# An attention kernel in which SyncE, not ScalarE, sends the rows of the maximum, the loop over pairs of images is written out, and the projections stand earlier

## What is computed

```python
h = group_norm(x) * gamma + beta                 # 32 groups of 4 channels
q, k, v = wq @ h + bq, wk @ h + bk, wv @ h + bv  # 128 x 1024 each
w = softmax(q.T @ k * scale, axis=-1)            # 1024 x 1024
x = x + wo @ (v @ w.T) + bo
```

## Time and profile before

| | us |
|---|---|
| median of 3 runs | 2451.29 |
| lowest and highest run | 2448.13, 2462.1 |
| the profiled execution's own time | 2444.07 |
| its span, first to last instruction | 2442.4 |

### The profile page before, as it was taken

How to read it: one execution, slowest core, us unless ns; L and a number is a source line. 1 busy time by engine, 2 the same in 40 slices (tenths; PEclk the granted TensorE clock), 3 DMA queues, 4 the chain that set the end, 5 groups by cost and what they waited for, 6 DMA issues and landing times. The chain is left out here.

```text
span 2442.4 us, 32992 instructions
## 1 busy us (share of the span) xinstructions
PE 2197.5 (90%) x11778; PEld 1067.0 (44%) x11778; DVE 1726.8 (71%) x2115; ACT 1661.2 (68%) x3009; POOL 458.7 (19%) x682
## 2 busy tenths in 40 slices
PE   1899899989998898999899988999887999999999
PEld 0333333333333333333333333333333888888887
DVE  0777768767776767677677867676752777777776
ACT  0366667656666666666666666676665888888887
POOL 4102020111202020201112020201101333333331
PEclk7789889989989998989899988998996999999999
DMA  7224151505234251605053351515101111111111
GB/s 143 29 47 69 37 81 38 90 23 83 45 60 62 44 76 30 97 21 90 25 80 54 51 72 33 85 34 91 25 16 47 57 41 63 62 54 40 62 50 46
DMA packets 63660, 137.36 MB, mean 56 GB/s; under 512 B 14880, under 2 KB 26272, under 8 KB 63392
## 3 DMA queue, kind: packets, MB, share of 16 engines
q1 hardware_dynamic: 60064, 133.90, 29.8%
q10 hardware_dynamic: 3456, 1.57, 0.4%
HBM read 57.31 MB, written 22.02 MB: 32 GB/s over the span
## 5 line engine op out<-in xcount | busy, mean ns | idle before, releaser
L473 DVE TENSOR_REDUCE h_half_nmax<-h_s_ps 128x2 f32<-128x1024 f32 x1024 | 1207.1, 1220 | 382.7 <-PE h_s_ps L660 378.4
L591 ACT ACTIVATE h_probs<-h_st_ps 128x512 f32<-128x512 f32 x2048 | 1070.5, 601 | 480.5 <-PE h_st_ps L764 448.5
L764 PE MATMUL h_st_ps<-h_qrep,h_krep 51*128 51x512 f32 x2048 | 690.0, 505 | 132.9 <-ACT h_probs L591 112.7
L764 PEld LDWEIGHTS h_st_ps<-h_qrep,h_krep 51*128 51x128 f32 x2048 | 295.4, 198 | 721.9 <-ACT h_probs L591 522.1
L650 PE MATMUL h_pv<-h_probs,h_vT 128*32 128x512 f32 x4096 | 599.6, 660 | 0.0
L660 PE MATMUL h_s_ps<-h_krep,h_qrep 48*128 48x512 f32 x2048 | 399.4, 450 | 72.9 <-SPq L241 29.5
L660 PEld LDWEIGHTS h_s_ps<-h_krep,h_qrep 48*128 48x128 f32 x2048 | 211.4, 203 | 188.8 <-DVE h_half_nmax L473 92.2
L1288 PE MATMUL o_s<-o_k,o_q 128*128 128x512 f32 x768 | 223.8, 427 | 8.7 <-DVE o_q L1109 5.7
L366 POOL TENSOR_SCALAR h_nparts<-h_nmax 128x16 bf16<-128x16 f32 x64 | 16.3, 254 | 1035.7 <-DVE h_nmax L480 1035.7
L1288 PE MATMUL o_pv<-o_pT,o_vT 128*128 128x512 f32 x768 | 207.3, 406 | 0.8 <-ACTq L1215 0.8
L1103 DVE TENSOR_TENSOR o_pT<-o_t,o_pT 128x512 fp32r<-128x512 f32 x256 | 164.5, 685 | 46.9 <-ACT o_pT L1240 44.5
(11 more groups left out here) (106 smaller groups left out, 1239.1 us busy)
## 6 DMA issues: line engine op xcount, KB each, us to landing
h_krep<-h_kp SPq DMA_DIRECT2D x96, 256.0 KB, 8.7
h_qrep<-h_qp SPq DMA_DIRECT2D x192, 128.0 KB, 9.8
x_res<-out_dram SPq DMA_DIRECT2D x32, 512.0 KB, 3.4
num<-av SPq DMA_DIRECT2D x128, 64.0 KB
rrep<-rden_dram SPq DMA_DIRECT2D x16, 512.0 KB
out_dram<-o_y SPq DMA_DIRECT2D x16, 512.0 KB
h_x_in<-out_dram SPq DMA_DIRECT2D x15, 512.0 KB, 3.3
out_dram<-h_y SPq DMA_DIRECT2D x15, 512.0 KB, 2.6
```

What stands on the lines that cost most here:

```text
L473: reduce = nc.vector.tensor_reduce(half_nmax[:, c, th, :, pair % MP], s_ps[slot][:, :, :], AX.X, ALU.max, negate=True)
L591: nc.scalar.activation(probs[g % 2][:, j, :], st_ps[n % COLUMN_BANKS][:, :], ACT.Exp, scale=1.0 / CH ** 0.5).then_inc(columns_done, 1)
L764: nc.tensor.matmul(st_ps[n % COLUMN_BANKS][:, :], krep[par][part, quad * 2 + m, st * P:(st + 1) * P], qrep[par][part, th, quad * 2 + m, :] ...
```

## The change

- `max_rows` on ACT only copies `mrow` and signals `mrow_ready`. SP has a new `max_rows` that waits for this signal and issues the DMAs, four instead of two for each. SP calls it at four places of a unit: after `spread`, after `replicate`, and twice after the gather of quad 0.
- `qrep` is laid out as heads by 1024 queries (before: two halves of heads by 512), so `replicate` takes 6 instead of 12 DMAs for q, with the same bytes. `nparts` and `split_max` write the new order of the maxima.
- `K0, K1, Q0, Q1, MAX1` are 0, 2, 3, 4, 5 (before 3, 4, 6, 7, 5), `AVG` is 14 of the odd step (before 0 of the even step), and `invert` stands at `k == 6` (before 5). POOL splits k before the maxima of `th` 1 and q behind them.
- Layer 0 reads the images from `x`; the 8 copying DMAs are gone.
- The `Fori` loops of all five engines are Python loops: the program is written out. `one_head` is unchanged.

```diff
-    AVG, K0, K1, MAX1, Q0, Q1, V, MAX0, O = 0, 3, 4, 5, 6, 7, 8, 13, 14
+    K0, K1, Q0, Q1, MAX1, V, MAX0, O = 0, 2, 3, 4, 5, 8, 13, 14
+    AVG = 14
...
-                if s % 2 == 0 and k in (AVG, V, O):
+                if k in (V, O) if s % 2 == 0 else k == AVG and not (last and s == 3):
...
-        qrep = [sb(f"qrep{i}", [P, 2, HEADS // 2, HALF], F32R) for i in range(2)]
+        qrep = [sb(f"qrep{i}", [P, HEADS // 2, T], F32R) for i in range(2)]
...
-                sp.wait_ge(parts_ready, 2 * u + 1)
-                for term, part in enumerate((0, 0, 1)):
-                    for r in range(2):
-                        to, of = r * ROWS + term * CH, slice(r * ROWS, (r + 1) * ROWS)
-                        sp.dma_start(krep[par][to:to + CH, :, :].bitcast(F32),
-                                     parts["k"][of, part, :].bitcast(F32)).then_inc(rep_dma, 16)
-                sp.wait_ge(parts_ready, 2 * u + 2)
...
-                sp.wait_ge(rep_dma, 16 * 6 * TERMS)
+                for which, of, n, order in (("k", krep[par], 1, (0, 0, 1)), ("q", qrep[par], 2, (0, 1, 0))):
+                    sp.wait_ge(parts_ready, 2 * u + n)
+                    for term, part in enumerate(order):
+                        for r in range(2):
+                            to = r * ROWS + term * CH
+                            sp.dma_start(of[to:to + CH, :, :].bitcast(F32),
+                                         parts[which][r * ROWS:(r + 1) * ROWS, part, :].bitcast(F32)).then_inc(rep_dma, 16)
+                sp.wait_ge(rep_dma, 16 * 4 * TERMS)
...
+            def max_rows(n, par, quad, th):
+
+                sp.wait_ge(mrow_ready, n)
+                for r in range(2):
+                    for m in range(2):
+                        of = (r * 2 + m) * MAX_PARTS * MP // 2
+                        sp.dma_start(qrep[par][r * ROWS + KS:r * ROWS + KM, quad * 2 + m, th * HALF:(th + 1) * HALF].bitcast(F32),
+                                     mrow[th][of:of + MAX_PARTS * MP // 2, :].bitcast(F32)).then_inc(mrow_dma, 16)
...
-            for b in range(B):
-                sp.dma_start(out[b, :, :], x[b, :, :]).then_inc(copy_dma, 16)
...
                         sp.wait_ge(rden_ready, u + 1)
                         spread()
+                    max_rows(4 * u + 1, u, 0, 1)
                     if not (last and u == 1):
                         replicate(1 - u, u)
+                    max_rows(4 * u + 2, u, 1, 0)
 
                     sp.wait_ge(y_ready, 2 * (u + 1))
...
                     kept["gather"](sp, 0, av_dma)
+                    max_rows(4 * u + 3, u, 1, 1)
+                    if not (last and u == 1):
+                        max_rows(4 * u + 4, 1 - u, 0, 0)
...
-            body(0, first=True)
-            with sp.Fori(1, PAIRS - 1) as pair:
-                body(pair)
-            body(PAIRS - 1, last=True)
+            for pair in range(PAIRS):
+                body(pair, pair == 0, pair == PAIRS - 1)
...
-                        if s % 2 == 0 and k == 5:
+                        if s % 2 == 0 and k == 6:
...
-            def max_rows(n, bank, step, th):
+            def max_rows(n, bank, th):
 
                 act.wait_ge(columns_ready, n)
                 own.done(nc.scalar.copy(mrow[th][:, :], st_ps[bank][:, :].bitcast(BF16)[0:MAX_PARTS * MH, 0:P]))
                 act.sem_inc(columns_done, 1)
-                par, quad = step // 2 % 2, step % 2
-                for r in range(2):
-                    act.dma_start(qrep[par][r * ROWS + KS:r * ROWS + KM, th, quad * 2:(quad + 1) * 2, :].bitcast(F32),
-                                  mrow[th][r * MAX_PARTS * MP:(r + 1) * MAX_PARTS * MP, :].bitcast(F32)).then_inc(mrow_dma, 16)
+                act.sem_inc(mrow_ready, 1)
...
                         if k % TILES == 0:
-                            pe.wait_ge(mrow_dma, 32 * (2 * s + k // TILES + 1))
+                            pe.wait_ge(mrow_dma, 64 * (2 * s + k // TILES + 1))
```

More of the change, by code:

```diff
@@ L171, in many_heads @@
         idle = sb("idle", [P, 2])
-        nparts = [sb(f"nparts{i}", [P, 2, MAX_PARTS, MP], BF16) for i in range(2)]
+        nparts = [sb(f"nparts{i}", [P, 2, 2, MAX_PARTS, MP // 2], BF16) for i in range(2)]
         mrow = [sb(f"mrow{i}", [MAX_PARTS * MH, P], F32R) for i in range(2)]
@@ L308, in body @@
                     else:
-                        load_g(out[(i + 2) % B, :, :], (i + 2) // B, NW if last else NG)
+                        load_g(image(i + 2), (i + 2) // B, NW if last else NG)
                     sp.dma_start(wo[:, :], w[i // B, :, W_P:W_P + NO]).then_inc(load_dma, 16)
@@ L381, in _ @@
             pool.sem_inc(nmax_ready, -1)
+            coefficients(1)
+            pool.sem_inc(coef_ready, -2)
             own.drain()
@@ L384, in body @@
                 for u in range(2):
-                    coefficients(u)
-                    split_max(4 * u + 1, 1)
                     if not (last and u == 1):
@@ L389, in body @@
                         split(2 * u + 1, "k")
+                    split_max(4 * u + 1, 1)
+                    if not (last and u == 1):
                         split(2 * u + 2, "q")
@@ L405, in body @@
                 own.drain()
-            body(first=True)
-            with pool.Fori(1, PAIRS - 1):
-                body()
-            body(last=True)
+            for pair in range(PAIRS):
+                body(pair == 0, pair == PAIRS - 1)
         @block.vector
@@ L497, in _ @@
                 statistics(part)
+            coefficients(3 + 2 * LEAD, 0)
+            dve.sem_inc(rows_ready, -(3 + 2 * LEAD))
             own.wait()
@@ L520, in body @@
                             n = order[s, k, "other"]
-                            if k == AVG:
-                                coefficients(n + 1, n % ROW_SLOTS, *((NEXT_EPS, True) if last and u == 1 else ()))
+                            if s % 2 == 1:
+                                coefficients(n + 1, n % ROW_SLOTS, *((NEXT_EPS, True) if last else ()))
                             elif k == V:
@@ L531, in body @@
                 own.drain()
-            body(first=True)
-            with dve.Fori(1, PAIRS - 1):
-                body()
-            body(last=True)
+            for pair in range(PAIRS):
+                body(pair == 0, pair == PAIRS - 1)
         @block.scalar
@@ L570, in _ @@
                 evacuate(n + 1, n % COLUMN_BANKS, which, c)
-            max_rows(5, 4 % COLUMN_BANKS, 0, 0)
+            max_rows(5, 4 % COLUMN_BANKS, 0)
             act.sem_inc(columns_ready, -5)
@@ L610, in body @@
                 own.drain()
-            body(first=True)
-            with act.Fori(1, PAIRS - 1):
-                body()
-            body(last=True)
+            for pair in range(PAIRS):
+                body(pair == 0, pair == PAIRS - 1)
             act.wait_ge(pv_done, 2)
@@ L732, in for_dve @@
                         pe.wait_ge(rows_done, n + 1)
-                        if k == AVG:
+                        if s % 2 == 1:
                             pe.wait_ge(stats_ready, u + 1)
-                            if last and u == 1:
+                            if last:
                                 combine_weights(nc, s_ps[slot][:, 0, :], wg)
@@ L791, in body @@
                 pe.sem_inc(attn_ready, -2)
-            body(first=True)
-            with pe.Fori(1, PAIRS - 1):
-                body()
-            body(last=True)
+            for pair in range(PAIRS):
+                body(pair == 0, pair == PAIRS - 1)
             columns, _ = places(True)
```

53 lines of the change are left out of this document (27 added, 26 removed).

## The result

The changed kernel took **2494.43 us** (median of 4 runs, 2480.15 to 2498.52), the kernel before in the same session 2449.71 us (4 runs, 2446.39 to 2462.1). The ratio is **1.0171, 95% interval 1.0120 to 1.0221**: slower by 1.7%, and the interval leaves open whether it is more than 2%. The two medians lie 44.7 us apart. The forecast was 2459 us with a range of 2415 to 2510. The profiled execution of the changed kernel took 2498.52 us, with a span of 2496.8.

What follows compares the result with a forecast made beforehand. PE, 90% busy, was taken as the bound, with stalls behind ACT. Middle units +17 us, first unit -13, prelude +3, last unit +1 gave +8 on 2444, 2452; the median lies 7 higher: 2459 us, range 2415 to 2510.

Steps and rivals of the forecast that it cites:

- the cost is not these issues but SP's order: SP's in-order queue delays the maximum rows, so PE stands 6.6 us at group 8 and 3.5 to 6 later.
- `rden` written: Even step: SP writes `rden` 21.5 us after the start, 0.2 us ahead of group 6 at 21.7.
- issues of the first rows: Even step, SP behind `spread`: four issues of about 0.73 us each, 2.9 us.
- `replicate`: Even step, SP behind the first rows: 29.5 us as in the prelude, less 0.3 for larger pieces of q.
- second rows, to PE's matmul: End of the even step, SP behind `replicate`: 3.8 us from first issue to last landing.
- odd step begins at: SP's chain makes the even step take 65.8 us, whatever PE does; PE alone would be there at 60.0.
- The middle units: 14 units: 65.8 us even plus 45.9 odd, 111.7 against 110.5, +1.2 each, +17 us together.
- The first unit: No `spread` and nothing earlier to project, so it keeps the gain: 98 us against 111, -13 us.
- The prelude: Start of the kernel: the average and coefficients of image 1 come at its end, +3 us.
- The bounds: Whole kernel, from varied issue, landing and clock costs: -34 to +65 us and more, given as 2425 to 2500.
- SP is in time: Rows arrive before PE needs them and 64 stalls go: 2355 us, or 2250 with unit 96.8; chance 0.14.
- The clock stays low: Low clock behind the longer stalls costs each odd step 5 us, not 2.2: +39, 2498 us; chance 0.13.

Runs made afterwards that it cites:

- `sp_sends`: The kernel before with the sends of maximum rows alone moved to SP, two DMAs each: 2369.69 us, ratio 0.9663.
- `invert5`: The changed kernel with DVE's `invert` one group earlier, back at group 5: 2428.15 us, ratio 0.9915 against the kernel before.
- `sp_sends_invert6`: The kernel before with its row sends moved to SP and `invert` one group later, at group 6: 2428.22 us, ratio 0.9904.
- `one_by_act`: The kernel before, loop written out, SP sending three row sets per unit and ACT those for the odd step's first half: 2271.59 us, ratio 0.9286.
- `sp_sends_written`: The kernel before with all row sends moved to SP, two DMAs each, and the loop written out: 2327.51 us, ratio 0.9508.
- `one_by_pool`: The kernel before, loop written out, SP sending three row sets per unit and POOL those for the odd step's first half: 2283.64 us, ratio 0.9348.

## Why the prediction was right, and where it was off

**The mechanism.** The sentence on which it rested, "the cost is not these issues but SP's order", held at each point at which it could be seen: two waits per unit at the two places named, 7.3 to 7.8 and 3.0 to 5.2 us where 6.6 and 3.5 to 6 were given; 179.6 us in all, over the 130 to 170 given; waits for ACT at 21 us, under 30; no idle of 4 us behind a branch; the rows directly behind `rrep`; the clock at 0.912, above 0.88. `sp_sends`, `invert5` and `sp_sends_invert6` show its lever: the step follows the chain's start one to one. The time itself was met less well: the median lies 35 us above the forecast, inside a range that is 95 us wide.

**The chain, term by term**, from the step's start, in the step shown above:

| term | predicted | measured |
|---|---|---|
| `rden` written | 21.5 | 22.3 |
| to the end of `spread` | 8.4 | 8.2 |
| issues of the first rows | 2.9 | 3.1 |
| `replicate` | 29.2 | 29.0 |
| second rows, to PE's matmul | 3.8 | 4.3 |
| odd step begins at | 65.8 | 66.9 |

**Where 35 us went.** The median came 35 us above the forecast, the profiled sum 46 us above mine (54 instead of 8). Most of it is in the middle units and in one omission.

- The middle units: +3.7 us each, not +1.2, together +35 us over my sum. The largest piece is the first line of the table, and it has two parts. Groups 0 to 5 take 21.96 us, not 21.7 (group 3, with Q0 behind the evacuation of K1, takes 4.2 and not 3.8). And `rden` is written 0.35 us behind the start of group 6 (444.45 against 444.10), not 0.2 ahead of it. Then the landing, 4.3 instead of 3.8, and `replicate`, 29.6 in the mean instead of 29.2. The odd step is 46.6, not 45.9.
- The first unit: -4.4 us, not -13. The step "27.1 + 24.5 + 43.7" left out that the first unit has a `replicate` too, with rows behind it. PE stands there as everywhere else:

```profile
150.74 0.80 PE L773 MATMUL h_st_ps<-h_qrep,h_krep 51*128 51x512 f32 x2 [6.33 <-DMA h_qrep<-h_mrow]
```

  That was an omission, not a mis-sized term: the even step ends 61.4 us into the unit and not at 51.6.
- The prelude +4.2 instead of +3, the last unit and what follows +2.6 instead of +1.

4.2 - 4.4 + 52.1 (the 14 middle units) + 2.6 = 54.5, and the span is 54.4 us longer.

The bounds hold a slip of their own: -34 and +65 us on the profiled 2444, with the 7 us to the median, give 2417 to 2516 us, not "2425 to 2500".

**The rivals.** *SP is in time* did not occur in the change, but with the chain started early and one set of rows taken off it, it nearly does: `one_by_act` at 99.4 us per unit stands near the 96.8 that I gave for it. So its price was near and its condition was what the change broke. *The clock stays low* gave 2498 us, and the total is close to that, but not by its mechanism: the mean clock of the middle units is 0.91 against 0.92 before, and the odd step is 0.7 us over my figure and not 2.8.

**The rule of the Trainium skill** (DMA: Bandwidth & Descriptors, "Issuing engines are not separate DMA queues"), that the choice of the issuing engine only saves its issue time, agrees with the traces where it speaks of the transfers: POOL's rows, sent beside SP's `replicate`, took 8.3 us to land. For the time of a kernel it is not enough. By it, giving one set of rows back to ACT could only cost ACT's issue time, some 1.5 us a unit; it took the written-out kernel from 2327.51 to 2271.59 us. What an engine waits for ahead of the issue decides.

**What the change would have had to be.** The three parts that I priced together come apart in the runs. Sends by SP: -79 us. The loop written out: -15, and -42 on top of the sends. All the rest (inversion a group later behind four projections, four issues instead of two, the average and coefficients moved, the input read directly): 2494.4 - 2327.5 = +167 us. The profiled spans are 171 us apart, and the traces of the change and of `sp_sends_written` say where:

- The even steps of the middle units are 9.5 us longer each, 133 in all. Of each 9.5, 6.7 are the later start of the chain (22.3 against 15.6): 3.8 for the inversion a group later, by `invert5`, and 2.9 for what else moved, in the main the projections ahead of it. The issues and landings of the larger number of row DMAs are 2.7 (3.1 and 4.3 us against 1.6 and 3.05).
- The odd steps are 0.8 us longer each, 11 in all.
- The start to the first column scores takes 4.2 us more, the first unit 2.6, the last even step 9.5.
- What follows the last even step takes 10 us more; in the last odd step PE's groups run at the low clock (4.1 us) from group 7 on, in `sp_sends_written` only from group 14 on.

Not tried was the change with its early projections placed behind `invert`, nor its smaller parts one by one, so what each part is worth alone is not shown.

## What to carry to other kernels

When a DMA is moved to an "idle" engine, write down what that engine waits for ahead of it, from which instruction that chain starts, and what in the same change moves that start; the idle share of the queue says nothing. If several waits hang on one chain, look at the last one first: here the first one moved ahead earned 9 us, the last one taken away 30 us in the change and 56 us in the written-out kernel, and one set of transfers sent from another queue did it. See also what comes in its place: four issues on ScalarE stopped the matmuls again, two did so less. Look at the clock behind a stall too: about half of what the best kernel gained in its middle units was the clock that stays up when the stalls go.

## What the runs showed of the hardware

- The cost of a stall in clock. With 148 us of PE idle in 1547 the middle units ran at 0.92 mean, with 75 us in 1391 at 0.99. Behind a wait of 3.0 us the clock was 0.50 for the whole 4.4 us of the window shown above.
- Landing of a small copy inside the chip's memory depends on what is under way: in `one_by_pool` 12 KB sent by POOL landed after a minimum of 2.1 us, in the last unit without `replicate`, and after a median of 8.3 and a maximum of 9.1 beside `replicate`'s 3 MB.
- The issue itself: 0.76 us a DMA on SP and on ACT for these shapes (3.06 / 4 and 1.52 / 2), 0.57 to 0.62 on POOL (2.27 / 4 and 1.23 / 2).
- Larger pieces did nothing for `replicate`: from its first issue to that of the rows behind it, the mean over the middle units is 29.5 us in `sp_sends_written` with q in 2 KB pieces and 29.6 in the change with 4 KB pieces and six DMAs fewer.
